# Fetching one unit in sixty-four by single rows from SyncE's queue, in a graph attention kernel

## The reference

```
n_in, n_out = x[recv], x[send]                     # recv = src, send = dst
wn_out = n_out @ W_lin + b_lin
e_ij   = leaky_relu2(concat(n_in, n_out) @ W_att + b_att)
a_ij   = e_ij @ w_alpha                            # one number for each edge
alpha  = softmax of a_ij over the edges of one receiver
n_i    = segment_sum(alpha * wn_out, recv)
out    = layernorm(x + elu(n_i))
```

## Time and profile before

| what | us |
|---|---|
| median of three timed executions | 2351.88 (2348.72 to 2352.53) |
| the profiled execution | 2347.53 |
| its span, from the first to the last instruction | 2345.8 |
| TensorE busy | 2035.6 (87%) |
| VectorE busy | 1738.2 (74%) |
| GpSimd busy | 1630.6 (70%) |
| ScalarE busy | 1187.4 (51%) |

### The profile page before, as it was taken

How to read it: one execution, slowest core, us unless ns; L and a number is a source line. 1 busy time by engine, 2 the same in 40 slices (tenths; PEclk the granted TensorE clock), 3 DMA queues, 4 the chain that set the end, 5 groups by cost and what they waited for, 6 DMA issues and landing times.

```text
span 2345.8 us, 58190 instructions
## 1 busy us (share of the span) xinstructions
PE 2035.6 (87%) x13268; PEld 1481.5 (63%) x13475; DVE 1738.2 (74%) x5298; ACT 1187.4 (51%) x3734; POOL 1630.6 (70%) x1697
## 2 busy tenths in 40 slices
PE   4629999999989999999979999999999999999990
PEld 2316666667666667666757666676666666666660
DVE  8847887777759877777768887777776666566667
ACT  3414466665546555555545455555455445454445
POOL 2027777777777777777777777777777777777760
PEclk9869999999999999999999999999999999999995
DMA  3125555554555555555555455555555555555541
GB/s 109 50 76 131 131 130 129 130 133 128 131 138 134 128 132 129 131 130 132 133 129 130 129 133 129 133 130 131 130 130 135 132 134 132 133 132 134 134 117 55
DMA packets 160607, 293.77 MB, mean 125 GB/s; under 512 B 37394, under 2 KB 104206, under 8 KB 160297
## 3 DMA queue, kind: packets, MB, share of 16 engines
q0 software_dynamic: 80064, 219.32, 36.9%
q1 hardware_dynamic: 79501, 70.44, 11.6%
q10 hardware_dynamic: 732, 0.27, 0.1%
HBM read 278.88 MB, written 11.02 MB: 124 GB/s over the span
## 4 chain that ended last, share of the span: by engine, by line
PE 56%; DMA 17%; DVE 10%; issue 8%; POOL 7%; ACT 1%; DVEq 1%; POOLq 0%; ACTq 0%
PE hidden_ps L901 17%; DMA rows<-qv_table,index 16%; PE masked_ps L912 12%; PE turned_ps L927 11%; POOL rows L583 7%; PE turned_ps L919 7%; PE hidden_ps L898 6%; DVE keys L1089 2%; DVE sums L1476 2%; DVE keys L1090 2%; DVE leaky L1432 1%; PE masked_ps L911 1%; DVEq L1476 1%; PE hidden_ps L820 1%; DMA w<-in_L_gnn_W_lin 0%
## 5 line engine op out<-in xcount | busy, mean ns | idle before, releaser
L583 POOL DMA_INDIRECT rows<-qv_table,index x1660 | 1602.3, 965 | 517.9 <-issue 473.9
L701 ACT ACTIVATE spare<-masked_ps,peaks 128x128 f32<-128x128 f32 x1660 | 473.3, 369 | 531.9 <-DVE peaks L1454 525.0
L901 PE MATMUL hidden_ps<-onehotT,p_part 128*128 128x128 bf16 x4980 | 707.5, 221 | 12.1 <-issue 0.5
L1476 DVE SCALAR_TENSOR_TENSOR sums<-sums,shrink,turned_ps 128x129 f32 x1660 | 574.3, 346 | 81.2 <-issue 21.8
L901 PEld LDWEIGHTS hidden_ps<-onehotT,p_part 128*128 x4980 | 464.9, 96 | 247.5 <-issue 182.1
L1439 DVE TENSOR_REDUCE lows<-masked_ps 128x4 f32<-128x512 f32 x415 | 286.2, 690 | 446.9 <-PE masked_ps L912 445.8
L927 PEld LDWEIGHTS turned_ps<-rows,spare 128*128 128x128 f32 x3320 | 451.5, 193 | 255.5 <-ACT spare L716 193.6
L898 PE MATMUL hidden_ps<-identf,rows 128*128 128x128 f32 x1660 | 469.5, 283 | 122.8 <-DMA rows<-qv_table,index 112.2
L927 PE MATMUL turned_ps<-rows,spare 128*128 128x129 f32 x3320 | 472.5, 279 | 27.1 <-DVE sums L1476 22.8
L912 PE MATMUL masked_ps<-leaky,w_cols 128*128 128x512 f32 x830 | 444.4, 618 | 14.9 <-issue 5.0
L691 ACT ACTIVATE sloped<-hidden_ps 128x512 f32<-128x512 f32 x415 | 248.5, 599 | 367.0 <-PE hidden_ps L901 363.9
(11 more groups left out here) (192 smaller groups left out, 833.3 us busy)
## 6 DMA issues: line engine op xcount, KB each, us to landing
lanes_all<-lane_list SPq DMA_DIRECT2D x415, 128.0 KB
rows<-qv_table,index POOLq DMA_INDIRECT x1660
qv_table<-rows SPq DMA_DIRECT2D x24, 257.0 KB, 2.6
out<-x_sb SPq DMA_DIRECT2D x1, 1344.0 KB
out<-x_sb SPq DMA_DIRECT2D x1, 896.0 KB
kept<-windows SPq DMA_DIRECT2D x3, 232.0 KB
keys<-in_src SPq DMA_DIRECT2D x2, 232.0 KB
keys<-in_dst SPq DMA_DIRECT2D x2, 232.0 KB
```

Source lines behind the costliest of these rows:

```text
L583: g.indirect_dma_start(out=rows[:, k % U, c, :], out_offset=None, in_=table, in_offset=bass.IndirectOffsetOnAxis(ap=index[:, k % U, c:c + ...
L701: last = a.activation(weightsT[:, k % 2, unit], masked_ps[:, k % 2, unit], ACT.Exp, bias=peaks[:, at + 2 * n:at + 2 * n + 1])
L901: mm = t.matmul(whole[:, unit], p_parts[s][:, bass.ds(of[c], F)], onehotT[:, k % 4, unit], start=False, stop=(s == 2), skip_group_check=True)
L1476: v.scalar_tensor_tensor(out=at, in0=at, scalar=shrink[:, k % 4, i:i + 1], in1=unit_sums_ps[:, i, :], op0=ALU.mult, op1=ALU.add).then_inc( ...
```

## The change

In every sixteenth chunk (15, 31, ..., 399: 25 chunks) the fourth unit is no longer gathered by POOL. SyncE fetches its 128 rows with 128 separate DMAs of one row each into a buffer of its own (`single_rows`, two places). It issues eight of them in each of the sixteen chunks before the unit is used, up to that chunk itself, behind `lanes_of(k)` and `besides(k)`. The row's address comes from a register; the registers are loaded four at a time from `single_at`, which VectorE makes from the sorted keys in `find_lanes` with two more instructions for each of the first three sets, and one for the last. TensorE waits for the fetched rows before such a chunk, and reads that unit from the new buffer. The ring of lanes has four places in place of two.

```diff
-    LANE_RING = 2
+    LANE_RING = 4
+    ROWS_EACH = 8
+    ROW_CHUNKS = -(-UNIT // ROWS_EACH)
+    RING_S = 2
+    COUNTS_S = 4
...
+    single_no = {k: n for n, k in enumerate(range(ROW_CHUNKS - 1, NCH, ROW_CHUNKS))}
+    single_of = {n: k for k, n in single_no.items()}
+    units_by_pool = {k: [c for c in range(C) if c < C - 1 or k not in single_no] for k in range(NCH)}
...
+        def fetched_in(n):
+            return fetched[n % COUNTS_S], (n // COUNTS_S + 1) * UNIT * 16
...
+            def fetch_rows(k):
+                n = k // ROW_CHUNKS
+                if n not in single_of:
+                    return
+                s, row = place(single_of[n])
+                first = k % ROW_CHUNKS * ROWS_EACH
+                if first == 0:
+                    sp.wait_ge(single_ready, s + 1)
+                    if n >= RING_S:
+                        sp.wait_ge(high_sums_done, single_of[n - RING_S] + 1)
+                for r in range(first, min(first + ROWS_EACH, UNIT), 4):
+                    starts = nc.values_load_multi_w_load_instructions(
+                        single_at[row:row + 1, s % 2, r:r + 4], engines=(mybir.EngineType.SP,), min_val=0,
+                        max_val=(PAD_ROW + P - 1) * R,
+                        skip_runtime_bounds_check_because="they are rows of the table, times the length of a row")[1]
+                    for i in range(4):
+                        sp.dma_start(single_rows[r + i:r + i + 1, n % RING_S, :],
+                                     flat_table[bass.ds(starts[i], R)].rearrange("(a r) -> a r", a=1)
+                                     ).then_inc(fetched_in(n)[0], 16)
+
             for k in range(NCH):
                 lanes_of(k)
                 besides(k)
+                fetch_rows(k)
...
-                for c in range(C):
+                for c in units_by_pool[k]:
                     g.indirect_dma_start(
...
-                    act.wait_ge(gathered[k % U], k // U * (16 * C))
+                    act.wait_ge(gathered[k % U], come[k - U])
...
-                pe.wait_ge(gathered[k % U], (k // U + 1) * (16 * C))
+                pe.wait_ge(gathered[k % U], come[k])
+                if k in single_no:
+                    pe.wait_ge(*fetched_in(single_no[k]))
...
-                    t.matmul(whole[:, unit], rows[:, k % U, c, 0:F], identf[:], is_transpose=True,
+                    t.matmul(whole[:, unit], rows_at_unit(k, c)[:, 0:F], identf[:], is_transpose=True,
...
+                    if s >= 2:
+                        dve.wait_ge(*fetched_in(max(n for k, n in single_no.items() if place(k)[0] == s - 2)))
+                    v.tensor_scalar(single_at[0:NO, s % 2, :], kept_i[0:NO, (PER - 1) * UNIT:PER * UNIT], (1 << SENDER_BITS) - 1,
+                                    None, ALU.bitwise_and).then_inc(single_found, 1)
+                    dve.wait_ge(single_found, s + 1)
+                    v.tensor_scalar(single_at[0:NO, s % 2, :], single_at[0:NO, s % 2, :], float(R), None,
+                                    ALU.mult).then_inc(single_ready, 1)
```

More of the change, by code:

```diff
@@ L134, in gnn_kernel @@
     X_LESS_AT = 100
+    single_no = {k: n for n, k in enumerate(range(ROW_CHUNKS - 1, NCH, ROW_CHUNKS))}
+    single_of = {n: k for k, n in single_no.items()}
+    units_by_pool = {k: [c for c in range(C) if c < C - 1 or k not in single_no] for k in range(NCH)}
+    come = [0] * NCH
+    for k in range(NCH):
+        come[k] = (come[k - U] if k >= U else 0) + 16 * len(units_by_pool[k])
     assert all(at + U + 2 < BEGIN[s] for at, s in senders_at.items())
@@ L157, in gnn_kernel @@
     table = nc.dram_tensor("qv_table", [(NB + 1) * P, R], F32, kind="Internal").ap()
+    flat_table = table.rearrange("n r -> (n r)")
     pads_dram = nc.dram_tensor("pads", [P, PC], F32, kind="Internal").ap()
@@ L194, in gnn_kernel @@
         sums = sb("sums", [P, NB, F + 1], F32)
+        single_at = sb("single_at", [P, 2, UNIT], I32)
+        single_rows = sb("single_rows", [P, RING_S, R], F32)
         keys_i = sb("keys", [P, 2, W], I32)
@@ L359, in gnn_kernel @@
         indexed = sem("indexed")
+        single_found = sem("single_found")
+        single_ready = sem("single_ready")
+        fetched = [sem(f"fetched{n}") for n in range(COUNTS_S)]
         gathered = [sem(f"gathered{r}") for r in range(U)]
@@ L410, in blocks_of, with rows_at_unit @@
                     for n in range(PER)]
+        def rows_at_unit(k, c):
+            if c == C - 1 and k in single_no:
+                return single_rows[:, single_no[k] % RING_S, :]
+            return rows[:, k % U, c, :]
+        def fetched_in(n):
+            return fetched[n % COUNTS_S], (n // COUNTS_S + 1) * UNIT * 16
         def place(k):
@@ L927, in unit_sums @@
                     mm = t.matmul(unit_sums_ps[:, c, :], weights[:, k % 2, c * P:(c + 1) * P],
-                                  rows[:, k % U, c, F:R], start=True, stop=True)
+                                  rows_at_unit(k, c)[:, F:R], start=True, stop=True)
                 mm.then_inc(done, 1)
@@ L1145, in find_lanes @@
                     v.tensor_tensor(lane_rows[:], lane_rows[:], bits[:], ALU.add).then_inc(lanes_ready, 1)
+                    dve.wait_ge(*fetched_in(max(n for k, n in single_no.items() if place(k)[0] == s - 2)))
+                    v.tensor_scalar(single_at[:, s % 2, :], kept_i[:, (PER - 1) * UNIT:PER * UNIT], float(R), None,
+                                    ALU.mult).then_inc(single_ready, 1)
             def columns_of(s):
```

## The result

The changed kernel takes 2320.1 us (median of four, 2318.1 to 2322.2) where before takes 2351.7: a ratio of 0.9862, 95% interval 0.9848 to 0.9876. The forecast was 2320. The profiled execution took 2322.19 us, span 2320.5.

A forecast was written before the change was run, and what follows sets the result against it. POOL's gather queue was taken as the bound, with SyncE's new work hidden beside it: 2351.9 - 31.8 for 25 gathers, with 0 added, gives 2320 us. The range was 2311 to 2410 us, the forecast's own 2312 to 2332.

The forecast's parts named there:

- POOL sets the pace, and a gather is worth its 1.27 us: POOL's queue: 25 gathers removed at 1.270 us each take 31.8 us off, last gather ending near 2248 us.
- TensorE can give up the time: TensorE, next behind POOL, gives up 1.6 us per 100 us from its waits for rows, leaving near 80 us.
- rival 1: TensorE takes over as bound and gives a third to all of the gain back: 2331 to 2352 us; chance 0.07.
- SyncE hides: SyncE's queue: 4.11 us a chunk beside POOL's 5.00, 0.89 us to spare, so the added work costs no time.
- A row DMA: SyncE, eight a chunk: 0.29 us start to start plus 0.08 us of register operations, 0.37 us each.
- A load of four words: SyncE's address loads, two a chunk: one access of 0.35 us each, under 0.5 us as a sign of being right.
- Rival 2: SyncE's row-DMA issue becomes the bound, costing 400 x (X - 5.08) us, X its time a chunk; chance 0.16.
- Rival 3: SyncE's loads go word by word, 2.4 us a chunk in place of 0.7: 2644 us; chance 0.08.
- The four places: Ring of lanes: by themselves 0 to 2 us of gain or loss; SyncE's lead of four chunks covers bursts.
- DMA engines: Single rows, possibly all on one engine: at most 2 x 55 ns each, 0.9 us a chunk, not a new bound.
- rival 4: One DMA engine saturates at 5.4 us a chunk, TensorE waiting for fetched rows: 2480 us; chance 0.04.
- SyncE's waits at L500: SyncE's wait at the lanes' DMA (L474 before): about 0.9 us a chunk, 370 us in all.

The follow-up runs named there:

- half_units: The changed kernel with every second single unit left to POOL, 13 units in place of 25: 2330.2 us against 2346.4 for before, ratio 0.9925.
- ten_rows_b: Against the changed kernel: ten rows a chunk (31 units), loads of sixteen, lanes' DMAs on ScalarE's queue; run beside the changed kernel on one chip: 2314.2 us, ratio 0.9827.
- ten_rows: Against the changed kernel: ten rows a chunk (31 units), loads of sixteen, lanes' DMAs on ScalarE's queue; first run: 2309.8 us against 2346.4 for before, ratio 0.9842.
- after_again: The changed kernel itself, run again for direct comparison on one chip: 2321.1 us, ratio 0.9866 of before.
- both_fetch_b: The changed kernel, but POOL gathers all four units again while SyncE still fetches its rows: 2346.7 us against 2348.4 for before, ratio 0.9994.
- loads_of_eight: The changed kernel, with one load of eight addresses a chunk in place of two of four: 2316.3 us, ratio 0.9861 of before.
- two_places_b: The changed kernel with two places for lanes in place of four, on a chip where POOL sets the pace: 2323.0 us against 2354.3 for before, ratio 0.9865.
- loads_of_two: The changed kernel, loading addresses two at a time in place of four: 3077.1 us where before takes 2345.3, ratio 1.312.
- places_only: The kernel before with only four places for lanes in place of two, on the slow chip (before 3310 us): 3311.3 us, ratio 1.0014.

## Why the prediction was right

**POOL sets the pace, and a gather is worth its 1.27 us.** Right. 13, 25 and 31 gathers gave 16.3 us (half_units), 31.6 us (the changed kernel) and 40.1 us (ten_rows_b against before, 2354.3 - 2314.2): 1.25, 1.26 and 1.29 us each. The other pairs spread more: 36.7 us for 31 gathers in ten_rows (1.18 each), 33.2 for 25 in after_again (1.33). With all gathers back the gain is 0.06% and not told from zero (both_fetch_b). The last gather was to end near 2248 us and ended at 2254.2: 1.9 us by the later start and 3.9 by the dearer mean. That the median came out at 2320.1 for a forecast of 2320 is luck in its last digits: the four runs of the changed kernel spread over 4.1 us, and the two profiled executions are 25.3 us apart and not 31.8.

**TensorE can give up the time.** Right: no sign of rival 1 at 25 gathers, nor at 31. The size of what is left was wrong: about 80 us of waits for rows were forecast, 99.7 are there, 94.1 to 100.1 in after_again, loads_of_eight and two_places_b, and 99.4 and 107.8 with 31 gathers fewer. So TensorE did not pay for the whole gain with its waits for rows. Where the rest came from was not resolved; its waits for VectorE at the sums went from 22.8 to 16.4 us.

**SyncE hides.** Right in the outcome, too cheap in the sum. Forecast were 4.11 us a chunk and 0.89 to spare; measured are 4.88 and 0.12. The terms:

- A row DMA: 0.37 forecast, 0.39 measured, + 0.02 x 8 = 0.2 us. The register work is two short operations, as taken, and the addressed DMA itself is no dearer (228 ns) than the plain ones of the earlier trace rows.
- A load of four words: 0.35 forecast, 0.551 measured, and about 0.04 around it: + 0.24 x 2 = 0.5 us. This is the term that was mis-sized. Four words were taken as one access, at little more than the 0.30 us of one word in the earlier trace rows, and that was the weak step. A load under 0.5 us was to be a sign of being right, and that sign failed.
- Stalls of the queue, not forecast: 4.88 - 4.80 = 0.1 us.

That it still fitted is in part luck: of 0.89 us to spare 0.12 were left, and another 0.015 us for each row DMA would have used them up.

The Trainium skill's 200 ns for each register loaded (Runtime: NRT & Kernel Launch, Instruction fetch mechanics) is too high for these loads from on-chip memory, where four take 138 ns each and sixteen 79, and too low for two, 371 each; the measurement decides.

**Rival 2's law** held about: X above POOL's pace costs 400 x (X - 5.08), 696 to 752 us for the 732 measured in loads_of_two. The changed kernel ended 0.12 us under the point at which it starts to cost.

**Rival 3** (word by word) did not happen for four words: 0.551 us in place of 1.20. The 0.741 us for two words may be two accesses, but no run has a load of one word on SyncE's queue, so this is not shown.

**The four places** cost and give nothing that was measured (places_only for before, on the slow chip alone; two_places_b for after). The lead that I counted on for the bursts was not needed. That POOL's eight chunks of buffers take up late lanes fits this, and was not tested by itself.

**DMA engines.** No sign of rival 4: the trace of the changed kernel has no wait of TensorE for fetched rows, and the queues moved as the bytes did, against the earlier trace rows:

```profile
q0 software_dynamic: 78864, 216.03, 36.2%
q1 hardware_dynamic: 85901, 73.74, 12.4%
```

The share of the second queue grew by what is about 80 ns for each of the 3200 rows ((0.124 x 2320.5 - 0.116 x 2345.8) x 16 / 3200), inside the 110 ns taken. No run shows through which of the sixteen engines the single rows went.

**SyncE's waits at L500**, 68.8 us in place of the 370 forecast, are the same miss as the sum for SyncE.

## What to carry to other kernels

Read an engine's pace from the start-to-start time of its instructions, not from its busy share: POOL was 70% busy and had no time to spare, and there a removed instruction is worth busy plus issue. Work moved to a free queue costs nothing up to the pace of the bound and nearly one for one beyond (732 us measured, 696 to 752 worked out), so measure the new queue's time for one turn of the loop and compare it with that pace. What is hidden on one chip may not be on another: where the engines paused between instructions, the same row DMAs cost 51 us and took the gain back.

## What the runs showed of the hardware

- Loading registers on SyncE from on-chip memory, by words in one load: 2 words 0.741 us, 4 words 0.551, 8 words 0.725, 16 words 1.257. Four words are cheaper than two. All loads of four and more begin at a multiple of 16 bytes from the row's start; half of the loads of two begin 8 bytes past one, and these are as dear as the others (median 0.743 and 0.731 us in the trace of loads_of_two).
- A DMA of 1028 bytes with a register address takes 0.228 us on SyncE's queue, and 0.39 from start to start with the two register operations that it needs.
- One chip of four ran the unchanged kernel in 3310 us in place of 2350, with POOL's gathers, TensorE's loads of a register (301 ns) and the DMA packets as fast as elsewhere, and pauses between instructions on POOL (2.3 us in the rows above), ScalarE (6.3), VectorE (5.6) and SyncE. TensorE's granted clock was 0.815 in place of 0.955. Its cause stays open.
